# Softmax sums through DRAM into 64 columns before the reciprocal, and extra 256-column matmuls in TensorE's planned waits

## The reference: what is computed

```python
x = x + layernorm(attention(layernorm(x)))          # 16 heads of 16, rotary positions, causal softmax, projection
x = x + layernorm(ffn(layernorm(x)))                # x @ U1 @ V1 + b1, gelu (tanh form), @ U2 @ V2 + b2, rank 64
```

```python
scores = jnp.einsum('bhid,bhjd->bhij', q, k) * scale
scores = jnp.where(causal, -jnp.inf, scores)
attn = jax.nn.softmax(scores, axis=-1)
out = jnp.einsum('bhij,bhjd->bhid', attn, v)
```

## Time and profile before

| | us |
|---|---|
| median of 3 runs | 1461.18 (1460.17 to 1464.87) |
| the profiled execution | 1475.42 |
| its span, first to last instruction | 1473.7 |
| mean granted TensorE clock in it | 0.891 |
| busy: TensorE, VectorE, ScalarE, GpSimd | 1321.4, 1129.2, 890.9, 626.1 |

### The profile page before, as it was taken

One profiled execution on the slowest core, in us unless ns is written; L12 is line 12 of the kernel. 1 busy time (PEld: TensorE's weight loads), 2 busy tenths in 40 slices (PEclk: granted clock), 3 DMA queues, 4 the chain that ended last, 5 costly groups with the idle time before them and its releaser, 6 DMA issues.

```text
span 1473.7 us, 29171 instructions
## 1 busy us (share of the span) xinstructions
PE 1321.4 (90%) x11888; PEld 584.0 (40%) x11888; DVE 1129.2 (77%) x1652; ACT 890.9 (60%) x1228; POOL 626.1 (42%) x564
## 2 busy tenths in 40 slices
PE   6689889989899989998999899889999989899995
PEld 2234334434434334343444344434343434345442
DVE  5688776779588878796678868887788687856856
ACT  4337565556466656665666666655566566777784
POOL 3363213842177216731483248422861131324444
PEclk9779678978799889998997999879998897999997
DMA  6735333455326643653466335743554345022322
GB/s 204 162 90 123 59 59 52 124 112 112 56 77 134 116 62 60 152 115 54 56 154 135 62 52 127 162 67 52 110 129 86 59 84 133 24 80 84 103 72 71
DMA packets 93066, 140.87 MB, mean 96 GB/s; under 512 B 19078, under 2 KB 55044, under 8 KB 92932
## 3 DMA queue, kind: packets, MB, share of 16 engines
q1 hardware_dynamic: 92932, 139.01, 44.7%
HBM read 70.79 MB, written 50.33 MB: 82 GB/s over the span
## 4 chain that ended last, share of the span: by engine, by line
PE 48%; DVE 17%; SPq 10%; DMA 10%; issue 6%; ACT 5%; POOL 3%; ACTq 0%; DVEq 0%; POOLq 0%
PE PV L1064 12%; PE RING L1046 8%; DMA SUM<-OT 8%; PE RING L1019 6%; SPq L886 5%; PE MI L983 5%; DVE SUM L1213 4%; DVE M L1192 4%; PE RING L1115 3%; PE MI L1074 3%; PE RING L1108 3%; DVE MB L1192 3%; ACT PB L1399 2%; DMA X<-x 2%; SPq L908 2%
## 5 line engine op out<-in xcount | busy, mean ns | idle before, releaser
L1399 ACT ACTIVATE PB<-RING 128x1024 f32<-128x1024 f32 (+2 forms) x640 | 586.6, 938 | 311.3 <-PE RING L1046 305.2
L1192 DVE TENSOR_REDUCE M<-RING 128x2 f32<-128x1024 f32 (+3 forms) x448 | 500.6, 1143 | 127.8 <-PE RING L1019 88.1
L1046 PE MATMUL RING<-QK 50*128 50x512 f32 (+3 forms) x1536 | 315.2, 443 | 45.0 <-DVE M L1192 17.6
L1019 PE MATMUL RING<-QK 48*128 48x512 f32 (+3 forms) x1536 | 305.4, 426 | 24.6 <-ACT PB L1399 10.9
L1472 POOL TENSOR_SCALAR_AFFINE_SELECT PB<-PB 128x512 f32<-128x512 f32 x256 | 164.7, 646 | 293.9 <-ACT PB L1399 293.7
L1064 PE MATMUL PV<-PB,VL 128*32 128x512 f32 (+3 forms) x2048 | 267.4, 610 | 15.7 <-ACT OT L1405 13.9
L1192 DVE TENSOR_REDUCE MB<-RING 128x2 f32<-128x768 f32 (+2 forms) x192 | 198.2, 1040 | 83.9 <-PE RING L1026 83.2
L1046 PEld LDWEIGHTS RING<-QK 50*128 50x128 f32 x1536 | 145.9, 201 | 265.5 <-DVE M L1192 97.9
L1019 PEld LDWEIGHTS RING<-QK 48*128 48x128 f32 x1536 | 159.2, 211 | 166.1 <-ACT PB L1399 93.4
L1477 POOL TENSOR_TENSOR ATT<-ATT,SUM 128x512 f32<-128x512 f32 x32 | 40.8, 1274 | 258.4 <-DVE SUM L1213 258.4
L1213 DVE RECIPROCAL SUM<-SUM 128x512 f32<-128x512 f32 x32 | 107.1, 3347 | 13.9 <-DMA SUM<-OT 13.7
(11 more groups left out here) (117 smaller groups left out, 1356.9 us busy)
## 6 DMA issues: line engine op xcount, KB each, us to landing
QK<-split_parts SPq DMA_DIRECT2D x372, 128.0 KB, 6.0
split_parts<-PARTS SPq DMA_DIRECT2D x60, 256.0 KB, 3.0
split_parts<-EO SPq DMA_DIRECT2D x60, 256.0 KB, 3.4
ATT<-OT SPq DMA_DIRECT2D x128, 64.0 KB, 2.6
block_mid<-Y SPq DMA_DIRECT2D x16, 512.0 KB, 9.5
F_X<-block_mid SPq DMA_DIRECT2D x16, 512.0 KB, 5.7
out<-F_Y SPq DMA_DIRECT2D x32, 256.0 KB, 2.2
X<-x SPq DMA_DIRECT2D x7, 1024.0 KB, 9.7
```

The costliest lines, as they stand in the source:

```text
L1019: ins = e.matmul(m[:, h, i, :], QK[g % 3][r, 0, k, 128 * t:128 * t + 128], QK[g % 3][r, 1, k, k0:k0 + n], start=(i == 0), stop=not open_en ...
L1046: ins = e.matmul(m[:, h, i, :], QK[g % 3][r, 1, k, 128 * j:128 * j + 128], QK[g % 3][r, 0, k, 512 * c + off:512 * c + 512], start=True, st ...
L1192: e.tensor_reduce(acc, ring(("max", g, s, u), pairs, n), AX.X, ALU.max).then_inc(v_max, 1)
L1399: e.activation(buf[:, :, pairs[0]:pairs[-1] + 1, :], ring(("score", g, s, u), pairs, n), ACT.Exp).then_inc(a_exp, 1)
```

## The change

The sums no longer travel as 16 equal copies. `att_load` sends one row of each sum to a DRAM tensor `head_sums` (2 DMAs in place of the 3 into SUM). After the four groups of a batch, for each c, `att_sums` gathers them into SUM[c], now [128, 2, 32]: each sum once, over all 128 partitions. `att_inverse` takes the reciprocal of these 64 columns, `att_out` writes them to the DRAM tensor `inverse_sums`, and `att_spread` reads that back into INV [128, 2, 512], 16 partitions for each head, in 2 DMAs. `att_scale` multiplies by INV, both halves k after the fourth group. Before, the halves k were inverted and scaled after two groups each. The planner learns the new steps, their costs and landing times.

The second part is in `order_of_work`: where TensorE has a planned wait, is in row mode, has seen a first `max`, has not planned the last one, and bank 0 is empty in the plan, it puts steps `again` into TensorE's list, one for each 180 ns of the wait over 60 ns. Each is one matmul of 48 rows and 256 columns from a QK that is loaded, into bank 0, and nobody reads it. It waits for the reader of bank 0's last user. The planned times of the other steps don't move by it.

```diff
@@ -164,8 +164,9 @@
             if j == 4 * c + 3:
                 z = t + LAG + 0.5
                 at += [(z, ("ot_copy", g, c)), (z + 0.5, ("att_load", g, c))]
-                if g % 2:
-                    at += [(z + 2.5, ("att_inverse", g // 4, c, g % 4 // 2)), (z + 3, ("att_scale", g // 4, c, g % 4 // 2))]
+                if g % 4 == 3:
+                    at += [(z + 1 + i / 2, (n, g // 4, c)) for i, n in enumerate(("att_sums", "att_inverse", "att_out", "att_spread"))]
+                    at += [(z + 3, ("att_scale", g // 4, c, k)) for k in range(2)]
         z = SLOTS * (g + 1) - LEAD
         at += [(z, ("chain_a", g)), (z, ("chain_b", g)), (z + 0.5, ("chain_turn", g)), (z + 0.5, ("shift", g))]
     at += [(t, (step[0] + "_out",) + step[1:]) for t, step in at if step[0] in TAKEN]
@@ -285,12 +286,16 @@
         return [("product", g, 3 if c == 0 else 11), ("att_load", g - 1 + c, 1 - c)]
     if what == "att_load":
         g, c = at
-        return [("ot_copy", g, c), ("att_scale", (g // 2 - 1) // 2, c, (g // 2 - 1) % 2), ("proj", g // 4 - 1, c, 2)]
-    if what == "att_inverse":
-        b, c, k = at
-        return [("att_load", 4 * b + 2 * k + 1, c)]
+        return [("ot_copy", g, c), ("att_inverse", g // 4 - 1, c), ("proj", g // 4 - 1, c, 2)]
+    if what in ("att_sums", "att_inverse", "att_out", "att_spread"):
+        b, c = at
+        last = (b, 0) if c else (b - 1, 1)
+        return {"att_sums": [("att_load", 4 * b + i, c) for i in range(4)] + [("att_spread", b - 1, c)],
+                "att_inverse": [("att_sums", b, c), ("att_out", b - 1, c)],
+                "att_out": [("att_inverse", b, c), ("att_scale", b - 1, c, 1)],
+                "att_spread": [("att_out", b, c), ("att_scale", *last, 1)]}[what]
     if what == "att_scale":
-        return [("att_inverse", *at)]
+        return [("att_spread", *at[:2])]
     if what == "proj":
         return [("att_scale", *at[:2], 1)]
     if what == "proj_out":
@@ -378,7 +385,7 @@
         ("DVE", "ln_stats ln_dev ln_shift max_out chain_a chain_b att_inverse proj_out fold_weights fold_out y_stats y_dev"
                 " y_shift f_zero f_weights f_stats f_rows f_u1_out f_y_out f_spread f_shift"),
         ("POOL", "ones ln_pow select att_scale y_pow residual f_pow f_ypow"),
-        ("SP", "load_x send load_group shift att_load store f_load f_fill f_rest f_next f_store")):
+        ("SP", "load_x send load_group shift att_load att_sums att_out att_spread store f_load f_fill f_rest f_next f_store")):
     TAKER.update(dict.fromkeys(names.split(), engine))
 
 
@@ -415,17 +422,21 @@
         "fold_weights": 900, "fold_out": 420, "y_stats": 420, "y_dev": 850, "y_shift": 400, "f_zero": 600, "f_weights": 2600,
         "f_stats": 2500, "f_rows": 1900, "f_u1_out": 1400, "f_y_out": 1530, "f_spread": 850, "f_shift": 170,
         "ones": 3700, "ln_pow": 1100, "select": 640, "y_pow": 1100, "residual": 1300, "f_pow": 1100, "f_ypow": 1050,
-        "rope": 2400, "round": 750, "rest": 2360, "att_scale": 1300, "att_inverse": 650, "f_norm": 1000, "f_res": 1250,
-        "load_x": 600, "send": 3300, "load_group": 5600, "shift": 2500, "store": 500, "att_load": 3000, "f_load": 5000, "f_fill": 3000,
+        "rope": 2400, "round": 750, "rest": 2360, "att_scale": 1300, "att_inverse": 550, "f_norm": 1000, "f_res": 1250,
+        "load_x": 600, "send": 3300, "load_group": 5600, "shift": 2500, "store": 500, "att_load": 2400, "att_sums": 600, "att_out": 600, "att_spread": 1200, "f_load": 5000, "f_fill": 3000,
         "f_rest": 2400, "f_next": 1200, "f_store": 600}
 LATE = {"PE": 270, "ACT": 160, "DVE": 60, "POOL": 60}
 
 MOVES = {"load_x": (1 << 20, 230, 4600), "send": (1 << 20, 230, 2700), "load_group": (3 << 19, 150, 3800),
-         "shift": (1 << 15, 150, 1500), "att_load": (5 << 16, 200, 1500), "store": (1 << 19, 230, 4200),
+         "shift": (1 << 15, 150, 1500), "att_load": (1 << 17, 200, 1500), "att_sums": (1 << 15, 150, 1500),
+         "att_out": (1 << 15, 150, 1500), "att_spread": (1 << 19, 200, 2500), "store": (1 << 19, 230, 4200),
          "f_load": (3 << 19, 230, 4600), "f_fill": (1 << 21, 230, 4600), "f_rest": (1 << 21, 230, 4600),
          "f_next": (1 << 20, 230, 4600), "f_store": (1 << 18, 230, 2500)}
 
 
+
+
+AGAIN, EVERY = 115, 180
 SWITCH, LOAD_ROWS, STAY, SLACK = 200, 100, 1.67, 0
 
 
@@ -451,12 +462,14 @@
         return 1060
     if what == "product":
         return 40 * width(at[1])[3] // 24 + 25
+    if what == "again":
+        return AGAIN
     return COST[what]
 
 
 def tiling(step):
 
-    return {"score": "rows", "max": "rows", "up": "rows", "f_y": "rows", "product": "columns", "down": "halves", "f_u1": "halves"}.get(
+    return {"score": "rows", "max": "rows", "again": "rows", "up": "rows", "f_y": "rows", "product": "columns", "down": "halves", "f_u1": "halves"}.get(
         step[0], "columns" if step[0] in ("qk", "values", "fold", "proj") else "whole")
 
 
@@ -478,7 +491,7 @@
 
     open_at, had = [0] * 7, {}
     bank, after, holds = {}, {}, {}
-    mode, moved = None, 0
+    mode, moved, latest, again = None, 0, None, 0
     last_max = max((s for s in due if s[0] == "max"), key=lambda s: (s[1], s[2], s[3]))
 
     def ready(step):
@@ -542,6 +555,14 @@
         assert best is not None, "the plan stands still"
         (start, _, q, banks), engine = best
         step = q.popleft()
+        if engine == "PE":
+            if step[0] == "max":
+                latest = step[1]
+            if mode == "rows" and latest is not None and last_max not in done and open_at[0] is not None and open_at[0] <= free["PE"]:
+                for _ in range(int((start - free["PE"] - 60) // EVERY)):
+                    again += 1
+                    order["PE"].append(("again", again, latest - (step == ("max", latest, 0, 0))))
+                    after[order["PE"][-1]] = [had[0]]
         took = cost(step)
         if engine == "PE":
             if tiling(step) != mode:
@@ -579,6 +600,7 @@
     EPS = 1e-5
 
     split = nc.dram_tensor("split_parts", (2, 2, 2, 16, 16, NT), fp32, kind="Internal").ap()
+    sums, inverse = (nc.dram_tensor(n, (2, 16, 512), fp32, kind="Internal").ap() for n in ("head_sums", "inverse_sums"))
     mid = nc.dram_tensor("block_mid", (NB * NT, D), fp32, kind="Internal").ap()
     x_rows = x.rearrange("b (t p) d -> b p t d", p=128)
     mid_rows = mid.rearrange("(c t p) d -> c p t d", p=128, t=4)
@@ -645,8 +667,10 @@
             X[1] = sb("X1", [128, 8, D])
             OT = sb("OT", [128, 512])
 
+
             ATT = [sb(f"ATT{c}", [128, 2, 512]) for c in range(2)]
-            SUM = [sb(f"SUM{c}", [128, 512]) for c in range(2)]
+            INV = sb("INV", [128, 2, 512])
+            SUM = [sb(f"SUM{c}", [128, 2, 32]) for c in range(2)]
             YS = [sb(f"Y{i}", [128, 4, D]) for i in range(2)]
             WP = sb("WP", [128, 2, D])
             BP = sb("BP", [128, D])
@@ -709,7 +733,8 @@
         s_ld = [sem(f"s_load{i}") for i in range(3)]
         s_sh = [sem(f"s_shift{i}") for i in range(3)]
         s_mid = [sem(f"s_mid{i}") for i in range(2)]
-        s_att = [sem(f"s_att{c}") for c in range(2)]
+        s_att, s_sum, s_inv = ([sem(f"s_{n}{c}") for c in range(2)] for n in ("att", "sums", "inverse"))
+        s_spread = sem("s_spread")
 
         v_half, v_one, v_pv0, v_bvw, v_mask = (sem(f"v_{n}") for n in ("half", "row", "pv_zero", "bias_wide", "mask"))
         a_cst = sem("a_consts")
@@ -899,15 +924,33 @@
                     g, c = at
                     k, r0 = g % 4 // 2, 64 * (g % 2)
                     w.wait_ge(a_ot, 2 * g + c + 1)
-                    if g >= 2:
-                        w.wait_ge(g_att, NTH["att_scale", (g // 2 - 1) // 2, c, (g // 2 - 1) % 2])
                     if g >= 4:
+                        w.wait_ge(v_inv, NTH["att_inverse", g // 4 - 1, c])
                         w.wait_ge(p_mi["proj"], NTH["proj", g // 4 - 1, c, 2])
                     w.wait_ge(v_mask, 1)
                     for r, p0 in ((0, 16), (32, 80)):
                         e.dma_start(ATT[c][r0 + r:r0 + r + 32, k, :], OT[p0:p0 + 32, :]).then_inc(s_att[c], 16)
-                    for r, p0, n in ((0, 0, 16), (16, 48, 32), (48, 112, 16)):
-                        e.dma_start(SUM[c][r0 + r:r0 + r + n, :], OT[p0:p0 + n, :]).then_inc(s_att[c], 16)
+                    for h, p0 in ((0, 0), (1, 48)):
+                        h0 = 4 * (g % 4) + h
+                        e.dma_start(sums[c, h0:h0 + 3:2, :], OT[p0:p0 + 65:64, :]).then_inc(s_att[c], 16)
+                elif what == "att_sums":
+                    b, c = at
+                    w.wait_ge(s_att[c], 64 * (4 * b + 4))
+                    e.dma_start(SUM[c][:, :, :], sums[c].rearrange("(k h) (j q) -> (h j) k q", k=2, q=32)).then_inc(s_sum[c], 16)
+                elif what == "att_out":
+                    b, c = at
+                    w.wait_ge(v_inv, NTH["att_inverse", b, c])
+                    if b:
```

(31 more changed lines are left out.)

## The result

| | before | changed |
|---|---|---|
| median, us | 1463.0 (1460.2 to 1468.8, 4 runs) | 1414.6 (1396.5 to 1420.3, 4 runs) |
| profiled execution, us (span) | 1475.4 (1473.7) | 1416.1 (1414.3) |
| mean granted clock | 0.891 | 0.946 |

The ratio is 0.962, with an interval of 0.953 to 0.972: 3.8% faster, 48 us between the medians. In the profiled executions it is 59 us, since the one of before was longer than its median. Ratios here leave out executions more than 1.5% over the fastest of their kernel, which leaves two of six in one case; where I give a mean of all, I say so.

A forecast was written before the change was run, and what follows sets the result against it. TensorE, 90% busy, was taken to set the pace, slowed by waits and the lower clock. Reciprocals -40, transfers -6 and extra matmuls -2 gave -48: 1427 us for the profiled execution, 1413 off the median, range 1380 to 1458.

The forecast's parts named there:

- The reciprocals, -40 us: VectorE's 32 wide reciprocals become 16 of 64 columns; fewer TensorE waits and lower-clock spells, 40 us less, ends 20 and 53.
- The bound of 52.8: TensorE behind reciprocals: 26.9 us of direct waits plus 25.9 us for 64.8 us of lower-clock spells, at 0.40 each.
- The transfers, -6 us: One DMA issue less ahead of ScalarE's copy of PV shortens 10 TensorE waits by 0.6 us each; between 0 and 14.
- several small waits: On TensorE, the 20-odd lower-clock spells without a reciprocal ahead were said to follow several small waits in one stretch.
- The extra matmuls, -2 us: 356 matmuls in TensorE's planned waits: 22 us too much, 26 us given back by the clock, 2 us waiting for bank 0.
- The sentence on the rule of the Trainium skill: On TensorE, same-row weight loads would not overlap matmuls, so extra matmuls take the higher price and the sum is 24 us worse.
- The price of the lower clock, 0.40: TensorE gets through 113 matmul records in 20 us instead of 189, so each lower-clock microsecond costs 0.40 us.
- The fourth rival: Sums' waits on SP hold seven shifts, SP standing still 10.5 us, each 6.4 us late: slower, 1477 us; chance 8%.
- Pieces of 128 B: Gather and write back of the sums in 128 B pieces might land 2.4 us later each, 34 us more in the fourth rival.
- Signs: What the profile after the change would show: expected VectorE time, waits for NS and the copy, extra matmul count, granted clock.

## Why the prediction was right, and where it was not

It said 1413 and the median is 1414.6. The terms behind it:

- **The reciprocals, -40 us.** Right in before's order: 39 us measured alone. The bound of 52.8, of which I took three quarters, was direct waits plus spells, and both showed, in other sizes: 26 us of direct waits where I counted 26.9, and 28 us less at the lower clock where I counted 65, read from an execution with 36 us more of it than the average. In the changed order the same reciprocals make up the gain otherwise: the wait for NS went, but others grew, and put back there they cost over 100 us. The number 40 belongs to before's order, and that the change as a whole came to much the same is not explained by it. The added 16 take 0.543 us, 0.5 said. What I gave as the reason beside it, that the plan's 650 ns made them dear, was wrong in kind: the true charge made the kernel slower.
- **The transfers, -6 us.** Wrong, as a term: one issue less was to shorten 10 waits by 0.6 each. ScalarE's wait for the landing went from 17.2 to 11.3 us, TensorE's for the copy only from 13.9 to 12.9. What I missed is the size of the whole matter. In the changed kernel the clock falls within 4 us of six of these waits, once for 30.7 us, and both together were worth 18 to 29 us when a second buffer took them away. In before the clock falls at 523.6, 677.2 and 987.8, each time 0.3 to 1.2 us after such a wait began and before it ended, so there the small waits ahead of it may have a part; no run gave before a second buffer. The prediction put these spells among those with "several small waits". The timeline of the changed kernel shows such a wait, and the window after it the clock:

```profile
938.28 0.60 ACT L1453 ACTIVATE OT<-PV 128x512 f32<-128x512 f32 x1 [1.12 <-DMA head_sums<-OT]
...
938.93 1.15 PE L1112 MATMUL PV<-PB,VL 128*32 128x512 f32 x8 [1.22 <-ACT OT L1453]
```

```profile
939.80:970.50 30.70, 30.70 (x199) 14.97 (x197) 14.14 (x18) 11.60 (x13) 5.60 (x7) 0.50 0.34 61
```

 How long such a spell lasts is not fixed. The other trace of the same program (span 1440.6 us) has 30.7 us at the lower clock from 350.7, where this one has 3.4 from 349.3, and 10.2 from 965.1, where this one has the 30.7 above. This is why the changed kernel's executions lie so far apart.

- **The extra matmuls, -2 us.** Right in sum in the changed order (0, within some 10), wrong in before's, for which it was worked out (10 us slower). It was off in three sizes. There are 475 of them and not 356: the prediction counted over the order of before and said that the count would hardly change; before with the extra matmuls has the 356, so the order's change added 119. What they give back was to be 66 us at the lower clock, thus 26 us; it is 12 us in the changed order, thus 5, and nothing in before's. What they take was to be 24 us (22 and 2) and is then about 5 in the changed order and 10 in before's. That the two sides cancel in the changed order, both a fifth of what was said, is luck as far as the sum goes. The price of one at full speed was right: from one extra matmul to the next 0.119 us (median of 217 at full clock) and 0.213 (25 at the lower), 0.12 and 0.215 said. The sentence on the rule of the Trainium skill can be decided now. Below are four of them, all in the same rows. Their matmuls start 0.12 us apart, and each has its own load of weights of 0.19 us.

```profile
648.92 0.66 PEld L1077 LDWEIGHTS MI<-QK 48*128 48x128 f32 x4
649.15 0.63 PE L1077 MATMUL MI<-QK 48*128 48x256 f32 x4
```

 "TensorE: Matmul & The Clock Gate" of the Trainium skill, Part 3 ("What overlaps and what doesn't"), has it that a load overlaps a running matmul only if the row groups differ. By the records the loads do run beside the matmuls here. Records of loads overlap one another as well, so what a load takes may be less than 0.19; but a matmul with its load comes at 0.119 us and not at the higher price, and with that goes the 24 us that the prediction named.
- **The price of the lower clock, 0.40.** One program's own executions measure it. For each I take the time at the lower level, (1 - clock) x 2 x span, against the span. A straight line through the ten executions of the changed kernel rises 0.46 us for each us at the lower clock, one through the 33 of before 0.30 (0.31 to 0.34 within one set). The 0.40 lies between. It can't be carried from one kernel to another: short reciprocals in before have 259 us at the lower clock on average, the changed kernel without extra matmuls 167, and both took 1417 us; in their traces the second waits 101 us where the first waits 76.
- **The fourth rival (the shift held on SP).** It came closer than 8% says, and didn't decide. In SP's list the three steps do all stand ahead of the shift, as the rival had it; here is the one of group 16 (timeline of SP):

```profile
642.73 1.03 SPq L935 DMA_DIRECT2D head_sums<-OT  x2
644.85 0.38 SPq L939 DMA_DIRECT2D SUM<-head_sums  x1
649.03 0.38 SPq L945 DMA_DIRECT2D inverse_sums<-SUM  x1
650.62 1.36 SPq L953 DMA_DIRECT2D INV<-inverse_sums  x2
653.40 2.48 SPq L921 DMA_DIRECT2D QK<-NSROW  x4
```

 SP is held from 643.8 to 652.0, 8.2 us for my 10.5, of which 4.2 lie between the issue of the gather and that of the write back: the landing, and the reciprocal behind VectorE's maxima. But ScalarE has the rows of the shift ready only at 653.4. At the seven such places the spread was issued 0.1 to 5.5 us ahead of that, five times by 0.8 to 1.4. I set the hold against the time to spare between shift and score, and left out the time between the landing of the sums and the chain's own end, which hides it. TensorE waited 2.1 us in 4 places for NSROW, and one spell of 3.4 us at the lower clock begins behind one of them.
 Pieces of 128 B didn't cost what I allowed for, either: what writes or reads head_sums lands in 1.8 us in the median, what writes or reads SUM in 1.7. The Trainium skill ("DMA: Bandwidth & Descriptors", specifications) gives 512 B as the least size for the full rate; a transfer of 32 KB in pieces of 128 B doesn't show a loss.
- **Signs.** Foretold: VectorE near 1030 us (1048), NS under 5 (1.2), some 350 extra matmuls (475), clock 0.92 to 0.93 (0.946), waits for the copy about 8 us (12.9). The clock was above the sign, and only a little of that is due to the extra matmuls: without them it is 0.941 on average, with them 0.945. The rest came with the new order of steps, since the short reciprocals in before's order have 0.909.

That the sum came out within 2 us owes much to chance. Measured by themselves the terms are 39 for the reciprocals, 0 for the extra matmuls and 0 to 10 for transfers and order together; the change as a whole was worth 48 us in the first set and 42 in the second. The 6 us for the transfers may be in there, but not as the shorter waits for the copy that they were meant to be, and the 40 are made up otherwise in the changed order.

## What to carry to other kernels

Where TensorE set the pace here, a single long operation on an engine that it waits for cost its wait and often a spell at the lower clock after it; look in the timeline at what stands just before each fall of the clock, and take that away first (here a long reciprocal, 39 us, and one missing buffer of 2 KB a partition, 18 to 29 us). Filling waits with matmuls that nobody reads raised the clock a little in one order (0.941 to 0.945) and the speed in none: measure the time, not the clock. A single trace can lie at the edge of what its kernel does (here 36 us more at the lower clock than the average), so check what you read from it against the clocks of the other executions. With an order that a planner writes, a change of one cost has a price of its own that may exceed the cost's (63 us here), so compare pieces of a change in a fixed order, and don't expect their worth to be the same in another (39 us and over 100 here).

## What the runs showed of the hardware

A tiny operation of VectorE can last as long as a big one of GpSimd. In the changed kernel L1206, over 4 columns, takes 0.17 us, but 2.15 in five of 16 places, each time ending with a GpSimd operation that had begun just before it:

```profile
592.61 2.15 DVE L1206 TENSOR_SCALAR VE<-MV 128x4 f32<-128x4 f32 x1
594.67 0.95 DVE L1240 TENSOR_REDUCE M<-RING 128x2 f32<-128x768 f32 x1
```

```profile
592.38 2.36 POOL L836 TENSOR_TENSOR EO<-EO,PARTS 128x1024 f32<-128x1024 f32 x1 [1.30 <-DVE PARTS L1218]
```

The maxima behind it are late, TensorE waits 1.54 us for M at 595.68, and the clock is down for 3.4 us from 598.4; five of the spells that are left begin like this. "SBUF — State Buffer" of the Trainium skill ("SBUF: two separate sides") describes such a thing: VectorE, in operations with two SBUF inputs or in a mode that uses two ports, shares a pair of ports with GpSimd, and whoever starts first keeps it for a whole instruction. That L1206 is in such a mode the trace doesn't show; its times agree (592.38 + 2.36 = 594.74, and 592.61 + 2.15 = 594.76); no run here tried another order of the two.
